# A decoder layer's attention in another matmul layout: bfloat16 score parts, two heads in two row halves, MLP by blocks, a new planner

## The reference

```python
# self-attention in latent form; W's fold into one query, one key, one value matrix
k_eff = (W_dq.T @ W_uq.T @ W_uk).reshape(nh, hs, n_kvl)
v_eff = transpose((W_uv.T @ W_o.T).reshape(n_kvl, nh, hs), (1, 0, 2))
attn = softmax(causal(q_lat @ c_kv.T / sqrt(hs)));  y = (attn @ c_kv) @ v_eff
x = layernorm(x + y)
# cross-attention over [ctx, x]: 512 memory keys, then 256 own keys, causal
q = x @ Wq;  k, v = split(concat(ctx, x) @ Wkv)
x = layernorm(x + softmax(mask(q @ k.T * d**-0.5)) @ v @ Wout + bout)
# 64 features, each with its own MLP of 16 inner units
s = x @ Win + bin_;  h = relu(s[..., None] * W1 + b1)
g = einsum('btmh,mh->btm', h, W2) + b2
x = layernorm(x + g @ Wout + bout)
```

## Time and profile before

| | us |
|---|---|
| median of 3 runs (lowest, highest) | 309.77 (309.51, 310.59) |
| the profiled execution: its span, which is its time here | 309.5 |
| TensorE (PE) busy | 277.4 |
| VectorE (DVE) busy | 234.5 |
| ScalarE (ACT) busy | 174.3 |
| GpSimd (POOL) busy | 72.6 |

### The profile page before, as it was taken

One profiled execution on the slowest core, in us unless ns is written; L12 is line 12 of the kernel. 1 busy time (PEld: TensorE's weight loads), 2 busy tenths in 40 slices (PEclk: granted clock), 3 DMA queues, 4 the chain that ended last, 5 costly groups with the idle time before them and its releaser, 6 DMA issues.

```text
span 309.5 us, 6148 instructions
## 1 busy us (share of the span) xinstructions
PE 277.4 (90%) x2240; PEld 181.3 (59%) x2240; DVE 234.5 (76%) x540; ACT 174.3 (56%) x365; POOL 72.6 (23%) x108
## 2 busy tenths in 40 slices
PE   4918678899999999999999999999999999999762
PEld 3706566576776657665656565665665666554431
DVE  2797716587775998888889878799778799777463
ACT  1520235456556567756667566776676658667430
POOL 8996601001202020301111211013101112112211
PEclk9985969999999999999999999999999999999795
DMA  6669999302034512120006200033000000000001
GB/s 188 243 190 303 258 300 229 137 3 55 4 124 85 175 35 102 54 103 3 1 2 162 48 1 2 1 86 71 2 3 2 2 2 1 3 2 17 2 18 34
DMA packets 16109, 23.64 MB, mean 76 GB/s; under 512 B 1648, under 2 KB 11824, under 8 KB 15952
## 3 DMA queue, kind: packets, MB, share of 16 engines
q1 hardware_dynamic: 13632, 14.19, 16.4%
q0 software_dynamic: 2160, 7.47, 8.0%
q10 hardware_dynamic: 288, 1.59, 1.4%
HBM read 13.02 MB, written 9.96 MB: 74 GB/s over the span
## 4 chain that ended last, share of the span: by engine, by line
PE 72%; DVE 17%; DMA 3%; issue 3%; SPq 1%; ACT 1%; POOL 0%; POOLq 0%; ACTq 0%; DVEq 0%
PE psum L1122 15%; PE psum L1104 13%; PE psum L1067 9%; PE psum L1075 7%; DVE pmax L869 5%; PE psum L1077 4%; PE psum L1130 4%; PE psum L1106 4%; DVE w2x L821 3%; DMA qm<-shift_rows 3%; PE psum L1084 3%; PE psum L1108 2%; DVE nmax_s L880 2%; DVE nmax_s L881 2%; PE psum L1159 1%
## 5 line engine op out<-in xcount | busy, mean ns | idle before, releaser
L735 ACT ACTIVATE probs<-psum 128x512 f32<-128x512 f32 x224 | 127.1, 594 | 61.0 <-PE psum L1104 36.1
L869 DVE TENSOR_REDUCE pmax<-psum 128x1 f32<-128x512 f32 (+2 forms) x176 | 111.9, 682 | 19.6 <-PE psum L1067 10.4
L1104 PE MATMUL psum<-qm,ks 98*128 98x512 f32 x176 | 79.9, 463 | 0.0
L1122 PE MATMUL psum<-probs,v 128*9 128x256 f32 (+1 forms) x1024 | 60.6, 354 | 0.0
L1075 PE MATMUL psum<-ks,qm 96*128 96x128 f32 (+1 forms) x256 | 51.0, 309 | 8.2 <-DVE probs L810 8.2
L1067 PE MATMUL psum<-ks,qm 96*128 96x512 f32 x128 | 52.6, 424 | 0.0
L1075 PEld LDWEIGHTS psum<-ks,qm 96*128 96x128 f32 x256 | 43.1, 202 | 13.1 <-issue 9.6
L866 DVE TENSOR_REDUCE nmax<-psum 128x2 f32<-128x512 f32 (+1 forms) x48 | 31.8, 687 | 18.4 <-PE psum L1077 18.3
L1104 PEld LDWEIGHTS psum<-qm,ks 98*128 98x128 f32 x176 | 33.1, 191 | 17.5 <-ACT probs L735 13.3
L669 POOL TENSOR_SCALAR_AFFINE_SELECT probs<-probs 128x512 f32<-128x512 f32 x32 | 19.7, 634 | 96.5 <-ACT probs L735 96.5
L1122 PEld LDWEIGHTS psum<-probs,v 128*9 128x9 f32 x1024 | 21.7, 90 | 31.2 <-issue 9.4
(11 more groups left out here) (133 smaller groups left out, 291.4 us busy)
## 6 DMA issues: line engine op xcount, KB each, us to landing
qm<-scr_q SPq DMA_DIRECT2D x28, 96.0 KB
ks<-scr_k SPq DMA_DIRECT2D x6, 384.0 KB, 4.4
ks<-scr_m POOLq DMA_DIRECT2D x2, 768.0 KB, 7.6
ks<-scr_m SPq DMA_DIRECT2D x2, 768.0 KB, 6.4
ctxT_sb<-ctxT ACTq DMA_DIRECT2D x1, 1024.0 KB, 8.2
scr_m<-probs POOLq DMA_DIRECT2D x2, 512.0 KB, 7.1
qm<-shift_rows SPq DMA_DIRECT2D x64, 4.0 KB
scr_k<-split_k SPq DMA_DIRECT2D x4, 256.0 KB, 2.0
```

What stands on the lines that cost most here:

```text
L735: nc.scalar.activation(probs[:, ring % PRING, h:h + nh, q0:T], src, ACT.Exp, scale=SCALE).then_inc(exp_done, 1)
L869: nc.vector.tensor_reduce(pmax[:, t % 2, col:col + nh, part], tile, axis=AX.X, op=ALU.max).then_inc(max_done, 1)
L1104: nc.tensor.matmul(tbank[n % TBANKS], keys, queries, start=True, stop=True).then_inc(scoresT_ready, 1)
L1122: last = nc.tensor.matmul(obank[t % OBANKS][32 * j:32 * j + HS + 1, q0:T], v, probs[:, pv_no[s] % PRING, j, q0:T], start=(kt == 0), stop=( ...
```

## The change

**Scores.** Each float32 operand is cut in three bfloat16 parts (high, middle, low). Six products of parts, for 8 head dimensions, make 48 rows of a contraction, and three rows more carry the three parts of the maximum (`ROWS` 51). One head lies in partitions 0 to 50, the other of its pair in 64 to 114. Every score matmul is issued as four, one for each column tile of 32, over 64 rows (`in_tiles`): 8 tiles of the array in all, the two heads of a pair in different banks. Causal masks are added by such tiles too (`mask`), over 64 rows of a small bfloat16 identity. Kind 1 and the own keys of kind 2 take one bank per head for maxima, with 384 columns to reduce; the memory keys one bank of 512 per head and query half, as before. Exponentials of kind 1 and of the own tiles leave out the half that is masked whole.

**Values.** Each values matmul of 128 rows becomes two of 64 rows that write two banks (`heads`, two banks wide); the drain copies both, and `norm`, now once for a unit instead of once for a step, adds them.

**Maxima.** One reduction of VectorE per step joins the pieces (`combined`); the three parts are split by four small GpSimd operations, the shift is a bfloat16 matmul with an identity, and for kind 1 the rows are sent by ScalarE's queue instead of SyncE's.

**Parts.** ScalarE makes the high part, VectorE the rest, GpSimd the middle and low ones (for the first, VectorE). Scratch writes are four DMAs for queries and keys of a unit together, and two DMAs read them back; `qk` holds four units, `km` the memory keys of all four batch elements.

**MLP by blocks.** 16 features to a strip of 32 partitions with a row of ones; `hid` multiplies a strip by a block of W1 (with b1 in the row of ones), so one relu of 512 columns follows; `g` multiplies by blocks of W2. `w2x`, the selection matrix and the feature split are gone.

**Banks and planner.** Six banks are given to any stage by the planner, two belong to the values. The planner knows four modes of the array ("tiles", "columns", "strips", "whole"), charges a switch between them, and fills pauses over 500 ns with matmuls of zeros (`warm`). At the start some matmuls of zeros are issued too.

```diff
-SLOTS = 3
-STACK = HG * SLOTS * HS
-ROWS = STACK + 2
+PARTS = 3
+SLOTS = 6
+STRIP = 32
+PAIRS = NH // 2
+HALF = P // 2
+DATA = SLOTS * HS
+ROWS = DATA + PARTS
-SBANKS, TBANKS, OBANKS, MBANKS = 3, 2, 1, 2
+FREE_BANKS = 6
+HEADS_BANK = 6
 PRING = 8
...
+COST = {"start": 9000, "s_ahead": 2200, "t_ahead": 1300, "slack": 60, "lat": 200, "switch": 110, "load": 90,
...
+def s_units(t):
+    own = [("own", j, 0) for j in range(HG)]
+    return own if kind(t) == 1 else [("mem", 2 * a + r, qt) for a in range(2) for qt in range(QT) for r in range(2)] + own
+def key_tiles(t):
+    return (0, 1) if kind(t) == 1 else (0, 1, 4, 5, 2, 3)
...
+def score_cols(s):
+    if s[0] == "S":
+        return (P + T + T, 3) if masked_before(s) else (MEM, 1)
+    cols = 2 * (T if own_tile(s[1], s[2]) != 1 else P)
+    return (cols + T, 3) if masked_before(s) else (cols, 2)
...
+            def in_tiles(o, lhs, rhs, start, stop):
+                for c in range(HG):
+                    last = nc.tensor.matmul(o[STRIP * c:STRIP * (c + 1)], lhs[:, STRIP * c:STRIP * (c + 1)], rhs, start=start,
+                                            stop=stop, skip_group_check=True)
                 return last
+            def mask(o, r, rows):
+                for c in range(HG):
+                    last = nc.tensor.matmul(o[STRIP * c:STRIP * (c + 1)], half(unit_b, r, HALF), half(rows, r, HALF)[:, c, :, :],
+                                            start=False, stop=True, skip_group_check=True)
+                return last
+            def score(s):
+                t = s[1]
+                g, u = group(t), unit(t)
+                src, j, qt = s_units(t)[s[2]]
+                p, r = 2 * g + j // 2, j % 2
+                queries, keys = (half(qk[:, u % B, p, a, :], r, DATA) for a in range(2))
+                m = bank_of(s)
+                if src == "mem":
+                    return in_tiles(m, queries[:, qt * P:(qt + 1) * P], half(km[:, u % B, p, :], r, DATA), True, True)
+                in_tiles(m[:, 0:P], queries[:, 0:P], keys[:, 0:P], True, False)
+                in_tiles(m[:, P:P + T], queries[:, P:T], keys, False, False)
+                return mask(own_blocks(m)[:, 0:3:2, :], r, neg)
+            def score_pair(s):
...
+                    last = in_tiles(m[:, a * (T - q0):(a + 1) * (T - q0)], keys, half(qk[:, u % B, p, 0, q0:], r, ROWS),
+                                    a == 0 or not masked, not masked)
...
+                        for h in range(2):
+                            last = nc.tensor.matmul(heads[STRIP * j:STRIP * j + HS + 1, h, q0:T], half(v, h, HALF),
+                                                    half(weights, h, HALF), start=(k == 0), stop=(k == len(key_tiles(t)) - 1))
...
+                    elif what == "norm":
+                        for qt in range(QT):
+                            for g in range(NG):
+                                for h in range(2):
+                                    last = nc.tensor.matmul(m[:, n * cols:(n + 1) * cols], headsT[:, at, h, qt * P:(qt + 1) * P],
+                                                            used_rows, start=(h == 0), stop=(h == 1))
...
+                    elif what == "hid":
+                        j = s[2]
+                        for k in range(2):
+                            inner = strip(wb_sb, j, FS + 1)[:, WB["w1"] + k * P:WB["w1"] + (k + 1) * P]
+                            last = nc.tensor.matmul(m[:, k * T:(k + 1) * T], inner, strip(s_sb, j, FS + 1), start=True, stop=True)
+                    elif what == "g":
+                        for k in range(2):
+                            for c in range(HG):
+                                f = 2 * c + k
+                                w2 = wb_sb[:, WB["w2"] + f * STRIP:WB["w2"] + (f + 1) * STRIP]
+                                last = nc.tensor.matmul(m[STRIP * c:STRIP * (c + 1), 0:T], w2, hid[:, f, :], start=(k == 0),
+                                                        stop=(k == 1))
...
+                    if src == "mem":
+                        nc.vector.tensor_reduce(pm[:, place, 1 + 4 * qt:2 + 4 * qt], m, axis=AX.X, op=ALU.max).then_inc(reduced, 1)
+                    else:
+                        nc.vector.tensor_reduce(pm[:, place, 2:5], own_blocks(m), axis=AX.X, op=ALU.max).then_inc(reduced, 1)
...
+                    nc.gpsimd.tensor_copy(high, full).then_inc(max_step, 1)
+                    nc.gpsimd.tensor_sub(rest, full, high).then_inc(max_step, 1)
+                    nc.gpsimd.tensor_copy(mid, rest).then_inc(max_step, 1)
+                    nc.gpsimd.tensor_sub(low, rest, mid).then_inc(max_split, 1)
```

More of the change, by code:

```diff
@@ new lines, in key_tiles, with own_tile, masked_before, masked_after @@
+def key_tiles(t):
+    return (0, 1) if kind(t) == 1 else (0, 1, 4, 5, 2, 3)
+def own_tile(t, k):
+    kt = key_tiles(t)[k] - (0 if kind(t) == 1 else MEM // P)
+    return kt if kt >= 0 else None
+def masked_before(s):
+    return s_units(s[1])[s[2]][0] == "own" if s[0] == "S" else kind(s[1]) == 1
+def masked_after(t, k):
+    return kind(t) == 2 and own_tile(t, k) is not None
+def rows_on_act(t):
+    return kind(t) == 1
+def low_on_dve(s):
+    return s == ("qk", 0)
+def mode_of(s):
+    return {"S": "tiles", "T": "tiles", "pv": "tiles", "shift": "columns", "hid": "strips", "g": "columns"}.get(s[0], "whole")
@@ L182, in ready, with slot_for, start_of @@
-        if what == "hidden" and s[2] and n < B - 1:
-            r = max(r, when(("hidden", n, s[2] - 1)) + COSTS["hidden_gap"])
-        return r
+        if what in ("ln1", "wo", "mo") and any(x[0] == "apply" for x in chain):
+            return NEVER
+        return when(*follows[what](*s[1:]))
+    def slot_for(s, start):
+        k = min(range(FREE_BANKS), key=lambda k: (max(free_at[k], start), free_at[k]))
+        return k, max(start, free_at[k])
+    def start_of(s, r=None):
+        r = ready(s) if r is None else r
+        if r == NEVER:
+            return r
+        start = pe_start(s, r)
+        return start if s[0] == "pv" else slot_for(s, start)[1]
@@ L302, in schedule @@
+    chain += [s for s, _ in LATE]
+    maxima = [("S", t, i) for t in range(STEPS) for i in range(len(s_units(t)))]
+    exps = [("T", t, k, r) for t in range(STEPS) for k in range(len(key_tiles(t))) for r in range(2)]
+    pvs = [("pv", t, k) for t in range(STEPS) for k in range(len(key_tiles(t)))]
     while maxima or exps or pvs or chain:
         now = free["pe"]
-        idle = [s for s in chain if s[0] not in MISC and ready(s) <= now + COSTS["slack"]]
+        step = maxima[0][1] if maxima else STEPS
+        idle = [s for s in chain if s[0] not in MISC and ready(s) <= now + COST["slack"]]
@@ L328, in schedule @@
[L328 to L338 removed]
+        best = []
```

1724 lines of the change are left out of this document (803 added, 921 removed).

## The result

| | before | after |
|---|---|---|
| median of 4 runs | 310.18 us (309.51 to 311.93) | 333.21 us (331.33 to 343.41) |
| profiled run, and its span | 309.77, 309.5 | 333.62, 331.9 |

The ratio is 1.070, 95% interval 1.063 to 1.076. Runs in which the chip granted a lower clock than in the kernel's best ones stand in the medians and ranges of this text, but not in its ratios; where most runs of a kernel were such, no ratio is given. The forecast was 265 us, within 238 to 312.

What follows compares the result with a forecast made beforehand. TensorE was taken to bound the kernel: 23 us of start, its 212 us of work less 8 outside the middle, divided by 0.93, and 23 us of end gave 265 us, within 238 to 312.

Steps and rivals of the forecast that it cites:

- the price of issue: TensorE's 6,400 pairs of weight load and matmul: issuing them was taken to add nothing beyond streaming.
- the issue rival: A TensorE pair costs a fixed time: 298 us at 25 ns, slower from 27 ns, 452 at 48; chance 0.13.
- The factor 0.93: Divisor on TensorE's middle work, a little under today's 0.95, since three engines now wait on each other.
- the 204 of the sum: TensorE's work between start and end: 212 us in all, less 8 outside this stretch.
- the falling clock: Sign of error: granted clock falls in the middle because TensorE now pauses; no size given.
- Norm: TensorE's product before the division: 256 records for 128, 0.09 us each, 23 us.
- The start: Stretch before the middle, 23 us; exponentials from about 29 us, 11 us earlier.
- the rival of serial halves: The two row halves take turns on TensorE: 65.5 + 56 us more, 385 us in total; chance 0.08.
- VectorE's reductions: Maxima in the middle: 128 at 0.617 us and 128 at 0.483, 141 us against 139 before.
- a step of kind 2 without a pause: Sign that the forecast is right: a kind 2 step of about 8.5 us for 10.2.
- ScalarE's sum of 198: ScalarE's whole work, exponentials, drains, splits, copies and row issues: about 198 us, from 174.
- Coupling: Shared banks and row latency keep VectorE at 0.86 or below: 277 us, or 293 at 0.80; chance 0.20.

Runs made afterwards that it cites:

- m1: TensorE alone, no layer computed: written-out rounds of matmuls on a constant tile, without waits, tiles of 512 and 128 columns and float32 values; 309.2 us in all.
- m2: TensorE alone on a constant tile: 768 matmuls of 64 rows by 32 columns, written out and as a loop of 64 per turn; 173.6 us in all.
- e2: Changed kernel with score columns cut finer, the same work in 1,792 more pairs of weight load and matmul; 383.9 us.
- e7: Changed kernel with values on all 128 rows in one bank, half the norm matmuls, and weights and values in bfloat16; 325.3 us.
- e10: e7 with every values matmul issued twice, 512 redundant pairs; 305.7 us, ratio 0.990 to the kernel before.
- e14: Changed kernel with a redundant bfloat16 matmul of 224 columns between every four records of norm's sums; 332.6 us, ratio 1.069 to the kernel before.
- e9: Changed kernel with norm reading only one of the two halves, 128 records for 256; 310.9 us, ratio 1.003 to the kernel before.
- e4: Changed kernel with first queries and keys written and read back ahead of the context load, and VectorE's identity cast after the first split; 330.3 us.
- e5: Changed kernel without its 768 mask matmuls; 317.9 us, ratio 1.027 to the kernel before.
- e8: Changed kernel with the weights and the values in bfloat16 instead of float32; 319.0 us, ratio 1.025 to the kernel before.
- e11: Changed kernel with values matmuls on 128 rows again but norm's 256 records kept; 328.2 us, ratio 1.052 to the kernel before.
- e3: Changed kernel with each unmasked score as one wide matmul instead of four of 32 columns; 344.2 us, ratio 1.104 to the kernel before.
- e13: Changed kernel with five banks in place of six for scores and the rest; 341.5 us, ratio 1.096 to the kernel before.

## Why the prediction was wrong

**The step that failed** is the price of issue, "I take the low end: the rows show no gap that only issue explains inside a group". It put the price at nothing. The rows were right and did not bear on it: eight loads within 0.03 us show how fast TensorE takes instructions that are there. Instructions come in blocks of 256 every 3.46 us at best, 27 ns a pair, and 4.3 us, 34 ns a pair, on the mean in this kernel. That the issue rival decides from 27 ns too is luck: its formula has every pair wait its turn (the 333.6 us would give ((333.6 - 46) x 0.96 - 82)/6,400 = 30 ns), while here short bursts pass and long ones stall. A row of the page before had the number to start from, 18 packets on the instruction queue for 4,480 TensorE instructions; I did not read it. The mechanism is shown by m1 and m2, and e2 shows that more of it costs more; in the kernel it is 25 us of waits instead of 4.5.

**The factor 0.93** is the term of the sum in which that price is missing, and the clock's with it. As a rough account, TensorE's busy 241.6 us at a clock of 0.86 are 208 us of full speed, for the 204 of the sum: the work as a whole was priced well. The factor gave these 204 us of work 219 us of time; the 208 took 276, that is 34 us of idle time, 25 of them waits on issue, and 34 us lost to the clock. So idle time, three quarters of it late instructions, is half of what was lost and the clock is the other half; the text had named the falling clock as a sign of error and put no price on it. e7 and e10 show that the clock moves such a kernel by 12 to 20 us, m2 that it falls where the stream pauses, e14 that it falls less when the sums are broken up.

**Norm** was sized at 0.09 a record, 23 us. Records start 0.11 us apart at full clock (in the kernel before too; of its four only the first two are closer, which made the 0.09) and 0.21 at half: the group is busy for 36.2 us.

```profile
L1108 PE MATMUL psum<-wa_sb,headsT 128*128 128x36 f32 x256 | 36.2, 310 | 0.0
```

With what goes with it in the clock, the half of it that the change added is worth 22 us (e9), all but one of the 23 by which the kernel is slower than before. This is the largest single term that an experiment took out. It does not make the late instructions harmless: e9 still waits 30.8 us on issue and only draws level.

**The start** was put at 23 us and came at 33.0. VectorE's casts, each of small tiles, took 2.86 and 3.01 us beside GpSimd's memsets, ahead of the first split:

```profile
9.57 2.86 DVE L836 CAST ident_b<-wa_sb 128x128 bf16<-128x128 f32 x1
9.65 3.01 DVE L838 CAST unit_b<-wa_sb 32x32 bf16<-32x32 f32 x2
```

and SyncE issued the first take at 23.0 us, behind the 1 MB context, x, the biases and four more writes, into full queues (DMA share 1.06 above); it landed ten microseconds later. The step "put 1.8 + 3.2 to land, take 0.9 + 4.4" left out the seven issues that stand between. The first exponential matmul came at 43.97 us, where 29 was forecast and the kernel before had 40.5. By e4's median the late start costs about 3 us at the end.

**Right:** the two row halves run side by side (m1: 0.228 us for eight tiles of 512), so the rival of serial halves is out; values are not dearer in halves (in m1 a round of four float32 tiles on 128 rows and one of eight on 64 take 0.43 us both); VectorE's reductions at 683 and 551 ns for 0.617 and 0.483 start to start, its sum 199 for 195; the end, 22.9 us for 23; a step of kind 2 without a pause, 7.3 us for 8.5. ScalarE's sum of 198 was too high: without the 14 to 19 for issues of rows, which the page's 167 does not count, it is still 12 or more above it.

**The rivals.** Coupling has part of the truth: VectorE waits 41.3 us for L1018 and 20.6 for L1011, which I put down to TensorE's pauses and clock; no run separates it. The issue rival, at a chance of 0.13, named the right term; it read "a pair costs a fixed time", where in fact pairs of a burst start 8 to 13 ns apart and the mean is bounded.

**Open:** how the 23 us divide between late instructions and the clock. They do not add up: e5 and e8 took packets away and half speed rose, e9 left the packets and half speed fell by 39 us. The marginal price of a packet was 3.2 to 4.1 us upward (e2), at most 2.6 and 1.8 downward (e5, e8, which also stream less), and 0.6 where the sums stayed (e11). Why e14's better clock buys no time is open too. Why e3 is slow was only argued.

## To carry to other kernels

Count TensorE's instructions before cutting matmuls into tiles: two for each record, 256 to a block, one block per 3.5 us at best (m1, m2) and 4.8 beside heavy DMA traffic (m1). A plan that keeps needing more than about 74 instructions per microsecond (256/3.46) will pause, and in m1 and m2 the clock fell with the pauses. Then look at what TensorE does between the dense parts: a block of narrow products in one piece was dearer than its records (e9), and less work meant more time where the clock hung by it (e7, e10).

## What the hardware showed unexpectedly

- Written-out TensorE code is bounded at 128 pairs per 3.46 us; the same matmuls in a loop of 128 instructions run at 13.3 ns each, and full clock.
- Tiles of 64 rows by 32 columns on 128 columns start 8 ns apart in bursts at full clock and 13 at half. The Trainium skill, "TensorE: Matmul & The Clock Gate", section "Wait — 56ns, not 53.3ns?", from which the prediction took a floor of 25 ns between starts, does not hold for them.
- Where 32 records of 36 columns in one piece (3.7 us) began at full clock, it fell in 15 of 19 cases (e11, e13 and the changed kernel), with 16 records in 1 of 21, and with wider matmuls between the 32 in 0 of 7.
- 512 redundant matmuls made a kernel 12 to 20 us faster (best runs 315.6 and 303.4, medians 325.3 and 305.7).
